# Moving the first top-16 tile into the last units of a local attention

## The chip, the cores and the metric

One core of one Trainium2 chip. The metric is the device time in microseconds of one execution of the whole kernel; below is better. The kernel is one program of five instruction queues: TensorE (PE in the profile; its weight loads are PEld), VectorE (DVE), ScalarE (ACT), GpSimd (POOL) and SyncE (SP), which wait for each other by semaphores set by hand.

## What is computed

Two batches of 1024 tokens with 256 features go through four blocks: a cross-attention, a mixture of experts, a global attention block with an MLP, and a last block. Only the last one matters here. Cut to its core:

```python
h = _ln(x) * (1 + sc_msa) + sh_msa
h = _self_attn(h, ...)            # windows of 128 tokens, rolled by 64; 16 heads of 16
x = x + h * g_msa
h = _ln(x) * (1 + sc_mca) + sh_mca
h = _topk_cross_attn(h, context, ...)
x = x + h * g_mca
h = _ln(x) * (1 + sc_mlp) + sh_mlp
x = x + _swiglu(h, ...) * g_mlp

# in _topk_cross_attn: 64 context tokens, 16 heads, TOPK = 16
scores = einsum('bqhd,bkhd->bhqk', q, k) / sqrt(D)
top_s, top_i = jax.lax.top_k(scores, TOPK)
attn = softmax(top_s); o = einsum('bhqk,bhqkd->bqhd', attn, vg)
```

## The kernel before, in words

A batch is two blocks of 512 tokens (k = 0, 1), each of four tiles of 128 tokens, so eight tiles t. PSUM has eight banks. Every engine's program is written out in its order by hand; an engine runs its instructions in that order, and a wait stops all that stands behind it on that engine.

**Local attention.** There are 16 units, u = 2 t + c: a window of 128 tokens and half of the heads. For a unit TensorE makes the scores minus the row maxima (`window_scores`, L1179 and L1182, banks 4 to 7), ScalarE their exponential (`window_exp`, L1710), TensorE the products with the values and the sums (`window_values(u - 1)`, L1197, banks 2 and 3), and VectorE divides (`window_divide`, L2312 and L2313). For units up to 6, token scores and row maxima of unit u + 9 (`window_tokens`, `window_maximum`) run between these. `window_scores(u)` waits for the exponential of unit u - 1; `window_values(u)` waits for its own exponential and for the division of unit u - 2.

When units 0 to 7 are divided, block 0 is complete. TensorE then multiplies it with the output weights (`projection`, L627 and L632, after the values of unit 8), VectorE adds it to x (`residual`, L1989) and takes mean and variance (`statistics`, L1895 to L1900) in its round 10, GpSimd takes the root (L2464), VectorE normalises (`normalise`, L1907) in round 11, TensorE turns the result (`ln`, L600) after unit 13, ScalarE evicts it with scale and shift (`ln`, L1412), and TensorE makes block 0's queries (`query`, L464) after unit 15's scores; ScalarE evicts those too. VectorE builds the key matrix of the top-16 attention (`build_keys(2)`, L2004 to L2007) in round 13. Block 1 goes the same way after the units.

**Top-16 attention.** For tile t, TensorE makes the scores against the block-diagonal keys (`top_scores`, L1254, banks 0 and 1); ScalarE copies them (`top_copy`, L1729) into one of the three buffers of `prob3`; VectorE takes the largest eight of each head with 16 MAX8 (`best`, L2346), marks them with 16 MATCH_REPLACE8 (`mark`, L2351), takes the next eight (`next_best`, L2358) and marks those (`mark_next`, L2363). Once the first are marked, GpSimd subtracts each head's maximum (`centre`, L2582), ScalarE takes the exponential (`exp`, L1733), and VectorE masks it with the marks (`mask`, L2369). TensorE turns the tile (`top_turn`, L1267), ScalarE evicts (`turned`, L1740), TensorE multiplies with the values (`top_values`, L1274), and VectorE divides (`divide`, L2014 and L2017), one tile later.

In the kernel before all of this comes after the units: VectorE's division of unit 15, then `best(0)`. Around tile 0 VectorE also has block 1's residual, statistics (after `mark(0)`) and normalisation (after `next_best(0)`), TensorE block 1's projection, turning and queries, and ScalarE their evictions, with `exp(0)` ahead of them and `exp(1)` behind.

`keep_busy(bank, n)` issues n matmuls of 128x512 whose result nobody reads (L592). From tile 4 on the MLP's matmuls are laced into the tiles (`up`, L1299, `down`, L1326); after tile 7 the second half of the MLP follows.

In SBUF `prob3` is three buffers of 4 KB; the first two lie over the second half of `kp3`, the keys that the units of block 1 read, the third lies behind it.

## Time and profile before

| | |
|---|---|
| three runs, median (lowest to highest) | 1666.86 us (1666.84 to 1670.57) |
| the profiled execution | 1668.83 us |
| its span, first to last instruction | 1666.8 us |
| PE busy, share of the span | 1526.9 us, 92% |
| DVE busy | 1048.8 us, 63% |
| ACT busy | 769.6 us, 46% |
| POOL busy | 379.3 us, 23% |
| chain that ended last, by engine | PE 68%, DVE 19%, issue 6%, ACT 4%, DMA 1%, POOL 1% |
| mean granted TensorE clock | 0.969 |

The chain is followed back from the last instruction, at each step to what released it; its shares say where the end was set, while busy time only says how full an engine is. "Issue" is time in which the engine waited for nothing that the profile shows. A busy PE is not PE at its peak. In batch 0 the units run from about 622 to 678 us and the tiles from 681 to 795 us; in batch 1 both come some 802 us later.

### The profile page before, as it was taken

The page shows a single profiled execution, that of the slowest core. Times are in us where ns is not written, and L with a number is a line of the kernel's source. Part 1 is how long each engine was busy: PE and PEld are TensorE (multiplying, and loading weights), DVE is VectorE, ACT ScalarE, POOL GpSimd, SP SyncE. Part 2 cuts the span into 40 slices and gives each one's busy share as a digit, 9 for nine tenths or more (in the row PEclk, how much of TensorE's full clock was granted, in tenths as well). Part 3 has the DMA queues.
Part 4 walks back from the last instruction along what each step waited for, and adds up shares of the span by engine and source line. Part 5 has one row for each costly group of instructions (what it writes and reads, how often), then busy time and mean ns, then how long its engine had stood idle before and what let it go on. Part 6 is the DMA issues. An engine that isn't in the chain of part 4 may idle for free.

```text
span 1666.8 us, 26374 instructions
## 1 busy us (share of the span) xinstructions
PE 1526.9 (92%) x10485; PEld 926.8 (56%) x10485; DVE 1048.8 (63%) x2946; ACT 769.6 (46%) x1228; POOL 379.3 (23%) x419
## 2 busy tenths in 40 slices
PE   5899998999998999878998999899999899987898
PEld 3447674444354857556764767444444475655676
DVE  3573344999627445899357334499982734579953
ACT  1334421688843533325443443148885354333444
POOL 3510006342016010114133000434400701001320
PEclk9899999999999999999999899999999999999999
DMA  9400017221020000000130000632202000000000
GB/s 336 143 1 0 0 41 147 36 40 26 2 76 1 1 1 3 1 1 1 56 109 1 0 1 0 161 49 40 40 2 77 1 1 1 3 1 1 1 1 26
DMA packets 37551, 59.60 MB, mean 36 GB/s; under 512 B 7360, under 2 KB 26980, under 8 KB 36532
## 3 DMA queue, kind: packets, MB, share of 16 engines
q1 hardware_dynamic: 25239, 34.71, 6.3%
q0 software_dynamic: 9408, 15.85, 6.2%
q10 hardware_dynamic: 2780, 7.36, 1.3%
q8 instruction: 82, 1.34, 0.3%
q14 instruction: 42, 0.34, 0.1%
HBM read 42.03 MB, written 2.10 MB: 26 GB/s over the span
## 4 chain that ended last, share of the span: by engine, by line
PE 68%; DVE 19%; issue 6%; ACT 4%; DMA 1%; POOL 1%; ACTq 0%; DVEq 0%; POOLq 0%
PE ps L993 9%; PE ps L1005 8%; PE ps L464 7%; PE ps L1299 4%; PE ps L978 3%; PE ps L870 3%; PE ps L1092 3%; DVE taken L2351 3%; PE ps L1100 3%; DVE rs L2036 2%; PE ps L848 2%; PE ps L592 2%; DVE mxw L2028 2%; PE ps L600 2%; PE ps L1156 2%
## 5 line engine op out<-in xcount | busy, mean ns | idle before, releaser
L2221 DVE TENSOR_REDUCE mm<-ps 128x1 f32<-128x1024 f32 x256 | 310.1, 1222 | 32.8 <-PE ps L978 25.6
L1618 ACT ACTIVATE pt<-ps 128x512 f32<-128x512 f32 x512 | 276.7, 600 | 59.1 <-PE ps L993 42.4
L2464 POOL TENSOR_TENSOR rstd<-ve,minus_half 128x4 f32<-128x4 f32 x32 | 35.7, 1114 | 745.0 <-DVE ve L1900 745.0
L993 PE MATMUL ps<-qx,kx 64*128 64x512 f32 x512 | 188.3, 445 | 1.0 <-ACT pt L1618 1.0
L978 PE MATMUL ps<-kx,qx 48*128 48x512 f32 x512 | 186.6, 444 | 0.2
L1005 PE MATMUL ps<-pt,v 128*32 128x256 f32 x2048 | 158.7, 390 | 0.0
L993 PEld LDWEIGHTS ps<-qx,kx 64*128 64x128 f32 x512 | 79.0, 184 | 95.9 <-ACT pt L1618 85.9
L2111 DVE TENSOR_TENSOR rlo<-ring,rhi 128x512 fp32r<-128x512 f32 x48 | 33.2, 692 | 121.6 <-ACT ring L1568 121.5
L1005 PEld LDWEIGHTS ps<-pt,v 128*32 128x32 f32 x2048 | 42.9, 108 | 85.5 <-ACT pt L1618 60.4
L978 PEld LDWEIGHTS ps<-kx,qx 48*128 48x128 f32 x512 | 75.4, 184 | 22.0 <-issue 18.0
L592 PE MATMUL ps<-filler 128*128 128x512 f32 x262 | 83.6, 434 | 0.0
L2510 POOL DMA_DIRECT2D qx<-mxT x64 | 33.3, 527 | 200.1 <-ACT mxT L1610 180.0
L1568 ACT ACTIVATE rhi<-ps,mod 128x512 fp32r<-128x512 f32 x48 | 33.0, 688 | 96.0 <-PE ps L779 95.9
L1989 DVE TENSOR_TENSOR x<-x,ps 128x512 f32<-128x512 f32 x64 | 41.3, 681 | 40.2 <-PE ps L616 27.5
L1412 ACT ACTIVATE hT<-ps,mod 128x512 f32<-128x512 f32 x48 | 34.7, 775 | 67.5 <-PE ps L600 67.5
L600 PE MATMUL ps<-ident,xhat 128*128 128x128 f32 x256 | 39.4, 296 | 26.9 <-DVE xhat L1907 23.6
L2305 DVE TENSOR_REDUCE mxw<-ps 128x8 f32<-128x1024 f32 x32 | 38.8, 1223 | 39.2 <-PE ps L1156 39.2
L2582 POOL TENSOR_TENSOR prob<-prob,m 128x1024 f32<-128x1024 f32 x16 | 31.0, 1936 | 142.5 <-DVE taken L2351 142.5
L1710 ACT ACTIVATE wprobT<-ps 128x1024 f32<-128x1024 f32 x32 | 32.7, 1023 | 61.1 <-PE ps L1182 60.9
L2028 DVE TENSOR_REDUCE mxw<-ps 128x16 f32<-128x1024 f32 x32 | 37.7, 1219 | 36.4 <-PE ps L650 36.4
L592 PEld LDWEIGHTS ps<-filler 128*128 128x128 f32 x262 | 44.8, 188 | 27.8 <-issue 22.3
L1907 DVE TENSOR_SCALAR xhat<-x,mv,rstd 128x256 f32<-128x256 f32 x128 | 46.3, 424 | 19.5 <-POOL rstd L2464 19.3
(373 smaller groups left out, 3397.5 us busy)
## 6 DMA issues: line engine op xcount, KB each, us to landing
wm<-in_L_xcond_W_mlp_dram SPq DMA_DIRECT2D x4, 1024.0 KB, 8.3
qx<-q_hi POOLq DMA_DIRECT2D x64, 64.0 KB, 2.6
kx<-k_hi POOLq DMA_DIRECT2D x64, 64.0 KB, 2.8
w3a<-in_L_xcond_w_m_dram SPq DMA_DIRECT2D x2, 2048.0 KB, 8.2
w<-in_L_xcond_e_w_dram SPq DMA_DIRECT2D x6, 512.0 KB, 6.9
w<-in_L_xcond_e_w_dram SPq DMA_DIRECT2D x2, 1536.0 KB, 13.6
s_ada<-in_L_xcond_w_ada_dram ACTq DMA_DIRECT2D x1, 2304.0 KB, 24.3
qx<-q_lo POOLq DMA_DIRECT2D x32, 64.0 KB, 2.6
```

The source lines that it names most:

```text
L464: ins = pe.matmul(ps[:, bank, :], w[:, c, m * P:(m + 1) * P], src[:, c, :], start=c == 0, stop=c == KC - 1)
L592: pe.matmul(ps[:, bank, :], filler[:, 0:P], filler[:, :], start=True, stop=True)
L600: ins = pe.transpose(ps[:, bank + c, t * P:(t + 1) * P], xhat[:, TB * k + t, c * P:(c + 1) * P], ident[:, :])
L870: ins = pe.matmul(ps[:, 6 - 2 * (j % 2) + c, :], w_[:, m, c * P:(c + 1) * P], part, start=n % 4 == 0 and i == 0, stop=n % 4 == 3 and i == 2)
L978: ins = pe.matmul(ps[:, bank + half, :], qx[r, p % 4, t * P:(t + 1) * P], kx[r, p % 4, half * 512:(half + 1) * 512], start=True, stop=True)
L993: pe.matmul(ps[:, bank, :], kx[r, p % 4, kc * P:(kc + 1) * P], qx[r, p % 4, half * 512:(half + 1) * 512], start=True, stop=True).then_inc( ...
L1005: ins = pe.matmul(ps[o:o + 32, 7, q:q + BLK // 2], v2[:, kc, VS * (2 * p + e):VS * (2 * p + e) + 32], pt[:, (2 * kc + e) % 8, half * BLK + ...
L1092: ins = pe.matmul(ps[:, m % 4, :], w1s[:, wp, c, m * P:(m + 1) * P], hs[:, k, sp, c, :], start=(wp, sp, c) == (0, 0, 0), stop=(sp, c) == ( ...
L1299: ins = pe.matmul(ps[:, 4 + i, :], w3ap[wp][:, c, (NC_HID * i + m) * P:(NC_HID * i + m + 1) * P], src[:, c, :], start=(wp, part, c) == (0, ...
L1618: act.activation(pt[:, u % 8, half * 512:(half + 1) * 512], ps[:, bank, :], ACT.Exp, scale=QK_SCALE).then_inc(st_read, 1)
L2028: ins = dve.tensor_reduce(mxw[:, t, :].rearrange("p (r n) -> p r n", r=4)[:, :, 0:4], ps[:, bank:bank + 4, o:o + D].rearrange("p r (h s) - ...
L2221: return dve.tensor_reduce(mm[:, p % 2, e, t:t + 1], place(), X, ALU.max).then_inc(ring_read, 1)
```

## The change

On TensorE: `top_scores` is defined ahead of the units. Block 0's projection stands ahead of `window_values(8)` in place of behind it, block 0's turning after unit 11 in place of 13, its queries after unit 12 in place of 15, and the scores of tile 0 after unit 13. After the units come the scores of tile 1, then block 1's projection, then the scores of tile 2; block 1's turning and queries stand behind the values of tile 0. Unread matmuls: 10 and 8 around block 1's projection, 5 and 4 around its turning, in place of 8 ahead of it, in bank 6 in place of 3.

On ScalarE: evictions follow, `top_copy(0)` stands after unit 13's exponential, and `exp(1)` ahead of the eviction of block 1's queries.

On VectorE: the rounds of the units end at 13. Block 0's residual and statistics come in round 9 ahead of the division of unit 8, the keys in round 8, the normalisation in round 10. Then `best(0)`; the division of unit 13; `mark(0)`; those of units 14 and 15; the rest of tile 0; block 1's residual and statistics after `mask(0)`, and its normalisation after `best(1)`.

On all: tile t lies in buffer (t + 2) % 3 of `prob3` in place of t % 3.

```diff
 # TensorE
                     window_scores(u)
                     if u + 9 < N_UNIT:
                         window_tokens(u + 9, 0)
+                    if u == 9:
+                        projection(R_B_SA, 0, wso, oT, 0, (None, (wo_ready, u0 + N_UNIT // 2), None))
                     if u:
                         window_values(u - 1)
                     if u + 9 < N_UNIT:
                         window_tokens(u + 9, 1)
                     if u == 7:
                         window_turn_maxima(1)
-                    elif u == 9:
-                        projection(R_B_SA, 0, wso, oT, 0, (None, (wo_ready, u0 + N_UNIT // 2), None))
+                    elif u == 11:
+                        ln(6, 0, bank=0)
+                    elif u == 12:
+                        query(2, 0, 14, wq3, bank=0)
                     elif u == 13:
-                        ln(6, 0, bank=0)
-                query(2, 0, 14, wq3, bank=0)
+                        top_scores(0)
                 window_values(N_UNIT - 1)
...
-                top_scores(0)
+                top_scores(1)
+                keep_busy(6, 10)
                 projection(R_B_SA, 1, wso, oT, 4, (None, (wo_ready, u0 + N_UNIT), None))
-                top_scores(1)
-                keep_busy(3, 8)
-                ln(6, 1)
-                query(2, 1, 14, wq3)
+                top_scores(2)
+                keep_busy(6, 8)
                 for t in range(TB):
                     if t:
                         top_scores(t + 2)
...
                     top_turn(t)
+                    top_values(t)
                     if t == 0:
-                        top_scores(2)
-                    top_values(t)
+                        keep_busy(6, 5)
+                        ln(6, 1)
+                        keep_busy(6, 4)
+                        query(2, 1, 14, wq3)
 # ScalarE
                     if u == 7:
                         window_maxima(1)
+                    elif u == 11:
+                        ln(6, 0, (mod, M3_SC_CA, M3_SH_CA), 0)
+                    elif u == 12:
+                        query(2, 0, C_BQ3C, 0)
                     elif u == 13:
-                        ln(6, 0, (mod, M3_SC_CA, M3_SH_CA), 0)
-                query(2, 0, C_BQ3C, 0)
+                        top_copy(0)
...
-                top_copy(0)
                 top_copy(1)
                 exp(0)
+                top_copy(2)
+                turned(0)
                 ln(6, 1, (mod, M3_SC_CA, M3_SH_CA))
+                exp(1)
                 query(2, 1, C_BQ3C)
-                turned(0)
-                top_copy(2)
                 for t in range(1, TB):
                     outputs3(t - 1)
-                    exp(t)
+                    if t > 1:
+                        exp(t)
                     top_copy(t + 2)
                     turned(t)
 # VectorE
-                for u in range(N_UNIT):
+                for u in range(N_UNIT - 2):
                     if u + 9 < N_UNIT:
                         window_maximum(u + 9)
+                    if u == 9:
+                        link(residual(5, 0, 0))
+                        statistics(b, 6, 0)
                     if u:
                         window_divide(u - 1)
-                    if u == 10:
-                        link(residual(5, 0, 0))
-                        statistics(b, 6, 0)
-                    elif u == 11:
+                    if u == 8:
+                        build_keys(2)
+                    elif u == 10:
                         normalise(b, 6, 0)
-                    elif u == 13:
-                        build_keys(2)
-                window_divide(N_UNIT - 1)
...
                     best(t)
                     if t == TB + 1:
                         add(0, 4)
+                    elif t == 0:
+                        window_divide(N_UNIT - 3)
+                    elif t == 1:
+                        normalise(b, 6, 1)
                     mark(t)
                     if t == 0:
-                        link(residual(5, 1))
-                        statistics(b, 6, 1)
+                        window_divide(N_UNIT - 2)
+                        window_divide(N_UNIT - 1)
...
                     next_best(t)
-                    if t == 0:
-                        normalise(b, 6, 1)
                     if t and t not in (TB, TB + 1):
                         divide(t - 1)
                     mark_next(t)
                     mask(t)
+                    if t == 0:
+                        link(residual(5, 1))
+                        statistics(b, 6, 1)
```

## Rows read from the trace of the kernel before

**Rows 1.** Busy time by stretch, VectorE alone: stretch, length, busy (instructions), clock, DMA, GB/s.
```profile
681.14:711.07 29.93, 28.59 (x212) 0.89 0.00 1
1483.00:1513.17 30.17, 28.58 (x211) 0.83 0.00 1
```
**Rows 2.** Waits of VectorE, 681 to 795 us: total us, times, longest.
```profile
DVE prob L2369 <- ACT prob L1733: 0.5, 1, 0.5
DVE rs L2014 <- PE ps L1274: 0.3, 1, 0.3
```
**Rows 3.** Timeline of VectorE, batch 0: start us, length us, instructions [idle before <-releaser].
```profile
660.79 0.96 DVE L2312 RECIPROCAL rs<-ps 128x128 f32<-128x128 f32 x1 [5.14 <-PE ps L1197]
...
661.99 1.27 DVE L1989 TENSOR_TENSOR x<-x,ps 128x512 f32<-128x512 f32 x2
...
665.22 0.95 DVE L2312 RECIPROCAL rs<-ps 128x128 f32<-128x128 f32 x1
...
670.12 1.28 DVE L2004 TENSOR_TENSOR kblk<-kT,head_mask 128x512 f32<-128x512 f32 x2
...
681.14 2.12 DVE L2346 MAX8 m<-prob 128x8 f32<-128x64 f32 x16 [1.77 <-ACT prob L1729]
...
718.73 0.26 DVE L2014 RECIPROCAL rs<-ps 128x16 f32<-128x16 f32 x1
```
**Rows 4.** Timeline of TensorE's matmuls, batch 0.
```profile
654.22 0.73 PE L627 MATMUL ps<-row_hl,row_of 64*128 64x512 f32 x2
...
658.54 0.50 PE L1179 MATMUL ps<-qT,kp 32*128 32x128 f32 x8
...
659.64 0.65 PE L1197 MATMUL ps<-wprobT,v 128*32 128x128 f32 x16
...
660.85 0.50 PE L1179 MATMUL ps<-qT,kp 32*128 32x128 f32 x8
...
673.31 3.70 PE L464 MATMUL ps<-hT,wq 128*128 128x512 f32 x8
...
677.96 1.98 PE L1254 MATMUL ps<-kblk,qT 128*128 128x512 f32 x4
...
685.40 2.42 PE L592 MATMUL ps<-filler 128*128 128x512 f32 x8
692.52 1.76 PE L600 MATMUL ps<-ident,xhat 128*128 128x128 f32 x8 [4.70 <-DVE xhat L1907]
695.15 6.06 PE L464 MATMUL ps<-hT,wq 128*128 128x512 f32 x8 [0.87 <-ACT hT L1412]
...
743.66 5.41 PE L632 MATMUL ps<-wco,oT 128*128 128x256 f32 x16
...
754.85 3.49 PE L1254 MATMUL ps<-kblk,qT 128*128 128x512 f32 x4
```
**Rows 5.** Timeline of ScalarE, batch 0.
```profile
679.98 1.03 ACT L1729 ACTIVATE prob<-ps 128x1024 f32<-128x1024 f32 x1 [2.24 <-PE ps L1254]
...
688.55 1.06 ACT L1733 ACTIVATE prob<-prob 128x1024 f32<-128x1024 f32 x1 [1.52 <-POOL prob L2582]
```
**Rows 6.** Timeline of all engines at an earlier projection, residual and norm.
```profile
485.09 3.72 PE L632 MATMUL ps<-wproj,hT 128*128 128x256 f32 x16
...
487.98 0.69 DVE L1989 TENSOR_TENSOR x<-x,ps 128x512 f32<-128x512 f32 x1 [0.70 <-PE ps L632]
...
489.57 1.38 DVE L1907 TENSOR_SCALAR xhat<-x,mv,rstd 128x256 f32<-128x256 f32 x4
...
491.48 1.08 ACT L1472 ACTIVATE hT<-ps 128x512 f32<-128x512 f32 x2 [10.49 <-PE ps L600]
```
**Rows 7.** Timeline of VectorE, a normalisation beside GpSimd's centring.
```profile
758.39 2.36 DVE L1907 TENSOR_SCALAR xhat<-x,mv,rstd 128x256 f32<-128x256 f32 x4
```
**Rows 8.** Busy time by stretch: stretch, length, busy of PE, PEld, DVE, ACT, POOL, clock.
```profile
640.00:680.00 40.00, 37.49 (x765) 27.82 (x764) 24.46 (x48) 14.59 (x17) 1.01 (x1) 1.00 0.01 2
...
692.00:702.00 10.00, 8.61 (x25) 4.56 (x26) 9.90 (x76) 2.88 (x5) 0.00 (x0) 0.66 0.00 1
```

More of the change, by code:

```diff
@@ L1199, in window_values, with top_scores @@
                     ins.then_inc(wpv_done, 1)
+                t0 = b * T
+                def top_scores(t):
+                    if t % TB == 0:
+                        pe.wait_ge(qT_ready, b * 2 * N_Q + 4 + t // TB + 1)
+                    if t == 0:
+                        pe.wait_ge(kblk_ready, b + 1)
+                    else:
+                        pe.wait_ge(ts_read, t0 + t)
+                    for c in range(KC):
+                        ins = pe.matmul(ps[:, c, :], qT[:, t // TB, c, t % TB * P:(t % TB + 1) * P],
+                                        kblk[:, c, :, :].rearrange("p h s -> p (h s)"), start=True, stop=True)
+                    ins.then_inc(ts_ready, 1)
                 window_linear(0, 0)
@@ L1234, in _ @@
                         window_turn_maxima(1)
-                    elif u == 9:
-                        projection(R_B_SA, 0, wso, oT, 0, (None, (wo_ready, u0 + N_UNIT // 2), None))
+                    elif u == 11:
+                        ln(6, 0, bank=0)
+                    elif u == 12:
+                        query(2, 0, 14, wq3, bank=0)
                     elif u == 13:
-                        ln(6, 0, bank=0)
-                query(2, 0, 14, wq3, bank=0)
+                        top_scores(0)
                 window_values(N_UNIT - 1)
-                t0 = b * T
-                def top_scores(t):
-                    if t % TB == 0:
-                        pe.wait_ge(qT_ready, b * 2 * N_Q + 4 + t // TB + 1)
-                    if t == 0:
-                        pe.wait_ge(kblk_ready, b + 1)
-                    else:
-                        pe.wait_ge(ts_read, t0 + t)
-                    for c in range(KC):
-                        ins = pe.matmul(ps[:, c, :], qT[:, t // TB, c, t % TB * P:(t % TB + 1) * P],
-                                        kblk[:, c, :, :].rearrange("p h s -> p (h s)"), start=True, stop=True)
-                    ins.then_inc(ts_ready, 1)
                 def top_turn(t):
@@ L1266, in top_turn @@
                         for j in range(4):
-                            ins = pe.transpose(ps[:, 2 + half, j * P:(j + 1) * P], prob3[:, t % 3, (4 * half + j) * P:(4 * half + j + 1) * P], ident[:, :])
+                            ins = pe.transpose(ps[:, 2 + half, j * P:(j + 1) * P], prob3[:, (t + 2) % 3, (4 * half + j) * P:(4 * half + j + 1) * P], ident[:, :])
                         ins.then_inc(tp_turned, 1)
@@ L1710, in window_exp, with top_copy @@
                     act.activation(wprobT[:, u % 2, :, :].rearrange("p (r o) q -> p r (o q)", o=2), ps[:, 4:8, 0:2 * P], ACT.Exp, scale=QK_SCALE).then_inc(wp_exp, 1)
+                t0 = b * T
+                def top_copy(t):
+                    act.wait_ge(ts_ready, t0 + t + 1)
+                    if t >= 3:
+                        act.wait_ge(tp_turned, 2 * t0 + 2 * t - 4)
+                    act.activation(prob3[:, (t + 2) % 3, :], ps[:, 0:2, :].rearrange("p a n -> p (a n)"), ACT.Copy).then_inc(ts_read, 1)
                 window_queries_keys(1)
@@ L2416, in _ @@
                     mask(t)
+                    if t == 0:
+                        link(residual(5, 1))
+                        statistics(b, 6, 1)
                 divide(7)
```

15 lines of the change are left out of this document (4 added, 11 removed).

## The prediction

> **What bounds the kernel now.** I read the chain of waits first: by its shares (in the table above) TensorE and VectorE set the time between them, so the question is which of the two sets the pace where the edits are. Then busy time by stretch, VectorE's waits, and each engine's timeline around the change. Each batch ends its local attention with sixteen units and then runs eight top-16 tiles on VectorE. Over the first two tiles (first selection of tile 0 to first selection of tile 2) VectorE is busy 28.6 us of 29.93 in batch 0 and of 30.17 in batch 1 [rows 1]; the remainder is overhead between instructions and few waits. From tile 0 to the end of tile 7 it has two other waits in batch 0, 0.5 us for the exponential of tile 1 and 0.3 us for tile 0's value products [rows 2]. So from tile 0 on VectorE is the path, and everything behind it (tiles 2 to 7, the MLP, the next batch) starts when it lets go. Ahead of tile 0 it is not: it idles 5.14 us before one unit's division [rows 3]. There TensorE and ScalarE are the path: scores, exponential, values, 2.31 us a unit (660.85 - 658.54) [rows 4].
>
> The gain is therefore the shift of one event, the first selection of tile 2 (711.07 us in batch 0). The shift has two parts: how much earlier tile 0 starts, and how much work VectorE gains or loses between there and tile 2.
>
> **When tile 0's scores come.** I walk TensorE's new order from the scores of unit 9, which nothing before the edit moves. Before, that unit's scores and the values of unit 8 precede the projection at 654.22, 2.2 us together, so they begin at about 652.1.
> - A half step (16 matmuls of scores or of values) is 1.10 us: scores at 658.54, values at 659.64 [rows 4]. The projection takes 4.32 us, from 654.22 to the next scores at 658.54.
> - Unit 9: scores to 653.2; the projection, now ahead of the values, to 657.5 (it needs unit 7's division, which follows that unit's values, issued before 652.1, by 1.15 us and lasts 1.20: done at about 653.3); values of unit 8 to 658.6.
> - Unit 10: bound by the exponential, 660.85 - 658.54 = 2.31, to 660.9. Unit 11: two half steps, to 663.1.
> - The norm's transposes, moved from unit 13 to unit 11. VectorE: the residual's first add starts 2.89 us into the projection's 16 matmuls (487.98 - 485.09) [rows 6], here about 656.8; adds and statistics 3.23 (665.22 - 661.99) [rows 3], to 660.0 and with the second add's wait 660.3; the divisions of units 8 and 9, 1.20 each, to 662.7; the normalisation's 1.38 ends at 664.1; 0.53 more to ScalarE's eviction (491.48 against 489.57 + 1.38) [rows 6]: 664.6. TensorE is free at 663.1 and needs about 1.0, so a new wait of 0.4 arises; the next scores start at 664.5.
> - Unit 12: two half steps and the query projection, 3.6 (its row has 3.70, of which the next instruction overlaps a little) [rows 4], to 670.3; ScalarE has evicted the norm's two halves by then. Unit 13: two half steps, 672.5; the top-16 scores, 2.02 to the copy's start (679.98 - 677.96), and 1.16 more to the selection (681.14 - 679.98) [rows 3 to 5]: **675.7**, where it was 681.14. Tile 0 starts 5.4 us earlier. The query's evictions and the copy lie between exponentials on ScalarE, which has over 1 us free in every unit.
>
> The added waits: the values of unit 10 want unit 8's division, done at 661.5, and come at 662.0, so 0.5 us is spare; the last unit's values want unit 13's division, which now stands behind tile 0's first selection, done at 679.1, when unit 15's exponential ends too. Building the keys (moved from unit 13 to unit 8) falls into VectorE's wait for the projection: 1.28 us and two small copies [rows 3] against 3.4 from 653.4 to 656.8. Without that wait it would cost its 1.6 once a batch on the norm's chain.
>
> **What VectorE carries until tile 2.** Three divisions (units 13, 14, 15), which were done before tile 0, now stand inside its chain: 3 x 1.20 = 3.6 us. Residual, statistics and normalisation of the second block only change places. The two waits of [rows 2] go, 0.8 us: tile 1's exponential no longer stands behind two query evictions, and tile 0's values come before the query matmuls. Batch 1 has 0.2 more to lose [rows 1]. From 675.7 the chain is 29.9 + 3.6 - 0.8 = 32.7, to 708.4 or 708.5.
> What must be on time there:
> - tile 0's exponential ended 8.5 us after the first selection's start (688.55 + 1.06) [rows 5]; with one division ahead that is 685.4, and the mask comes near 690.2;
> - the second projection starts when unit 15's division is done, 684.8, and takes 4.3, to 689.2; the residual comes at 691.4 (spare 2.2). Ten unread matmuls ahead of it, 8 of which took 2.42 [rows 4], end before 684.8 too;
> - tile 1's exponential, behind the norm's evictions on ScalarE, at about 704.4 against a mask at 707.4;
> - tile 0's values by 696.5, against their division at 703.6.
> Cost of all four: nothing, and each has 2 us or more to lose first. The query of block 1 now ends near 703.6. At half clock it would end near 706.1, the next tile's turn would slip to 711.3 and its values to 714.9; their division is due 7.66 us after tile 2's selection (718.73 - 711.07) [rows 3], at 716.1: still covered. Of the 27 unread matmuls (8 before), none is on the path then.
>
> **The sum.** Per batch 5.4 - 3.6 + 0.8 = 2.6 us, with 0.2 more in batch 1: 5.4; I take 5.3, by the later of the two readings of tile 2 above. The profiled execution took 1668.83 us for a span of 1666.8; it should become 1663.5. The median of the three runs is 1.97 below it, so by the median: 1666.86 - 5.3 = **1661.6 us**. Unknown ends: the new wait at the norm between 0 and 1.5 us a batch (VectorE's queue against TensorE's), the unit chain otherwise exact to 0.3; below, the two waits may stay (+0.8 a batch). That gives 1660.4 to 1664.8 for this case.
>
> **A collision.** The normalisation took 2.36 us where GpSimd ran the centring at the same time and 1.38 elsewhere [rows 6, 7]. In the new order the centring of tile 1 starts after the normalisation of block 1 (698.1 against 701.4), so I add nothing. The Trainium skill (GPSIMD Engine Reference, Key points) says the two engines share their SBUF interfaces, so that a VectorE instruction reading two SBUF inputs or in a two-port mode contends; the trace agrees. If both batches met it once, 1.0 us each, the sum would come to 1663.6.
>
> **Rivals.**
> - *Slower: the clock falls in the units.* TensorE was granted 1.00 of its clock through the units, and 0.66 in 692 to 702, right after it had idled 4.70 us [rows 4, 8]; the reordered units give it a new pause at the norm. At 1.2 GHz the query takes 6.06 instead of 3.70, the projection 5.41 instead of 3.72, the top-16 scores 3.49 instead of 1.98 [rows 4]: 2.4 + 1.7 + 1.5 = 5.6 us a batch, 1661.6 + 11.2 = 1672.8. It decides beyond a delay of 2.6 us a batch. Against it: the pause is 0.4 us, and TensorE keeps its 37.49 us of 40 or nearly in a stretch that was granted 1.00 [rows 8]. Chance 6%. The Trainium skill (TensorE: Matmul & The Clock Gate, What's actually happening) holds the throttled state to be the default and activity what releases it; by that rule any thinner stretch is a risk, and the trace agrees only for the long pause.
> - *The gain is mostly given back*: the divisions are paid in full but tile 0 starts only 3 to 4 us earlier, because the norm's chain through VectorE, GpSimd and ScalarE ends later than I say, or the collisions above occur. 1 to 3 us gained, 1664 to 1666. For it: six handovers between engines lie in that chain. Chance 27%.
> - *It does not shorten anything*: something behind tile 2 that VectorE's timeline does not show holds the end (a DMA, a split). Against it: VectorE has no wait in tiles 2 to 7. 1666.9, chance 6%.
> - *More*: the norm costs no wait and the second half of each batch meets a better clock, 7 us gained, 1659.9. Chance 8%.
> The forecast has 53%.
>
> **Numbers.** A change of 0.3% (5.0 us, below 1661.9) is about what measuring this kernel can tell from none, and the forecast sits just beyond it. Of its 53% I count 44 below that line, with 8 from the last rival: faster 0.52. Same: the rest, 0.41. Slower by over 0.3% (above 1671.9): the clock rival, with a point for the unforeseen, 0.07. The range leaves out the clock rival and half of both tails: 1659.5 to 1666.5.
>
> **What would show it.** In the new profile of batch 0: the first selection at 675 to 677; three divisions among tile 0's selection and marking; no wait of VectorE for an exponential or value product before tile 7; tile 2's first selection 2.2 to 2.8 us earlier, and the same shift at the end of tile 7; twice that at the end of the span. The forecast is wrong if the unit chain waits over 1 us for the norm, if VectorE waits inside tiles 0 and 1, or if the shift at tile 2 does not reach the end.

## The result and the profile after

| | before | after |
|---|---|---|
| median of 18 executions each | 1666.01 us | 1656.84 us |
| lowest to highest | 1660.26 to 1672.5 | 1650.26 to 1663.1 |
| the profiled execution, its span | 1668.83, 1666.8 | 1657.31, 1655.5 |
| mean granted TensorE clock in it | 0.969 | 0.978 |

The ratio is 0.995, with a 95% interval from 0.9938 to 0.9962: 8.3 us faster by the ratio, 9.2 by the medians. I had predicted 1661.6 us and a range that ended at 1659.5. The direction was right, the size was not, and the question of the experiments was where the 4.8 us beyond the forecast came from. Of these 0.9 are in the starting point: the kernel before has a median of 1666.01 us over 18 executions, and 1666.86 over the three that I had.

First the place that was edited. The timeline of VectorE around tile 0, batch 0, marks left out:

```profile
658.69 0.69 DVE L1998 TENSOR_TENSOR x<-x,ps 128x512 f32<-128x512 f32 x1 [1.82 <-PE ps L632]
...
664.59 1.37 DVE L1916 TENSOR_SCALAR xhat<-x,mv,rstd 128x256 f32<-128x256 f32 x4
...
677.43 2.12 DVE L2354 MAX8 m<-prob 128x8 f32<-128x64 f32 x16 [1.77 <-ACT prob L1723]
679.59 0.96 DVE L2321 RECIPROCAL rs<-ps 128x128 f32<-128x128 f32 x1
...
684.12 0.96 DVE L2321 RECIPROCAL rs<-ps 128x128 f32<-128x128 f32 x1
685.12 0.29 DVE L2322 TENSOR_TENSOR oT<-ps,rs 128x128 f32<-128x128 f32 x1
685.32 0.95 DVE L2321 RECIPROCAL rs<-ps 128x128 f32<-128x128 f32 x1
...
698.49 1.39 DVE L1916 TENSOR_SCALAR xhat<-x,mv,rstd 128x256 f32<-128x256 f32 x4
...
710.29 2.12 DVE L2354 MAX8 m<-prob 128x8 f32<-128x64 f32 x16
```

The three divisions stand inside tile 0's selection, and tile 2's first selection comes at 710.29. That can't be held against 711.07 [rows 3] as it is, because this execution reached the units 1.9 us later than the one of before did. A mark that no edit touches is needed: ScalarE's second copy of row maxima in a batch (`maxW`), at 649.06 us before (first line) and at 650.98 after (second):

```profile
649.06 0.60 ACT L1704 ACTIVATE maxW<-ps 128x512 f32<-128x512 f32 x1 [0.55 <-PE ps L1163]
650.98 0.60 ACT L1709 ACTIVATE maxW<-ps 128x512 f32<-128x512 f32 x1 [0.55 <-PE ps L1163]
```

From that copy to tile 0's selection it is 26.45 us (677.43 - 650.98) against 32.08, to tile 2's 59.31 against 62.01. I call this stretch the **zone**; it holds every edit. The busy time of VectorE by stretch, tile 0 to tile 2 in both batches, answers to [rows 1]; below it are its waits from tile 0 to tile 7, which answer to [rows 2] (batch 1 shows the same single line):

```profile
677.43:710.29 32.86, 32.12 (x218) 1.00 0.01 1
1469.01:1501.85 32.84, 32.10 (x217) 1.00 0.01 1
```

```profile
DVE m L2354 <- ACT prob L1723: 1.8, 1, 1.8
```

The one wait left is that for tile 0's scores, ahead of the stretch. TensorE's timeline answers to [rows 4]:

```profile
655.79 3.72 PE L632 MATMUL ps<-wso,oT 128*128 128x256 f32 x16
...
664.34 0.62 PE L1197 MATMUL ps<-wprobT,ones_win 128*32 128x128 f32 x16
665.05 1.41 PE L600 MATMUL ps<-ident,xhat 128*128 128x128 f32 x8
...
668.50 3.70 PE L464 MATMUL ps<-hT,wq 128*128 128x512 f32 x8
...
674.25 1.99 PE L1212 MATMUL ps<-kblk,qT 128*128 128x512 f32 x4
...
701.24 3.70 PE L464 MATMUL ps<-hT,wq 128*128 128x512 f32 x8
```

The norm's transposes wait for nothing, and the second query takes 3.70 us where it had taken 6.06. Last the whole span in stretches, all engines (length, busy of PE, PEld, DVE, ACT, POOL, granted clock, DMA share, GB/s): start to zone, zone, tiles 2 to 7, the stretch to the next zone, zone, and the rest.

```profile
0.00:650.98 650.98, 601.24 (x4057) 340.58 (x4057) 382.90 (x613) 304.81 (x508) 161.50 (x204) 0.97 0.20 55
650.98:710.29 59.31, 56.80 (x695) 39.51 (x695) 46.66 (x251) 21.68 (x26) 5.89 (x4) 1.00 0.01 2
710.29:791.36 81.07, 63.03 (x314) 47.62 (x315) 79.27 (x609) 34.28 (x47) 23.92 (x15) 0.96 0.00 1
791.36:1442.56 651.20, 618.43 (x4162) 362.18 (x4160) 389.43 (x574) 323.18 (x525) 151.45 (x174) 0.99 0.14 35
1442.56:1501.85 59.29, 56.77 (x695) 39.51 (x695) 46.63 (x250) 21.69 (x26) 5.88 (x4) 1.00 0.01 2
1501.85:1655.50 153.65, 127.97 (x602) 97.88 (x602) 104.49 (x654) 64.94 (x96) 30.24 (x19) 0.96 0.02 8
```

The stretch between the zones, from batch 0's last mask to batch 1's maxima copy, holds no edit, and took 658.80 us before:

```profile
792.11:1450.91 658.80, 625.95 (x4162) 366.04 (x4160) 389.31 (x574) 323.02 (x525) 151.72 (x174) 0.98 0.14 34
```

The same 4162 matmuls keep TensorE busy for 618.43 us instead of 625.95: 7.5 us less, the whole 7.6 of the stretch. So the profiled 11.3 us divide as follows: zones 2.70 + 2.97 = 5.67, between them 7.6, and 1.9 given back at the start, which had more half-clock time than before (41 us against 34).

The half-clock time of a stretch is the sum of the pieces in which the granted clock stood at 1.2 GHz instead of 2.4. It follows from the mean clock: 0.9895 over 651.2 us (rounded to 0.99 above) is 14 us of it, 0.9767 over 658.8 is 31.

### The profile page after: what moved, and what is told of

Its sections match the earlier page's. It is cut to its first block, busy times and chain, and to the rows that moved or that the text cites. A ratio compares the mean times of both kernels' runs of the same rounds, so it can differ in the third digit from the quotient of the medians.

```text
span 1655.5 us, 26452 instructions
## 1 busy us (share of the span) xinstructions
PE 1524.2 (92%) x10523; PEld 927.3 (56%) x10523; DVE 1049.4 (63%) x2946; ACT 770.6 (47%) x1228; POOL 378.9 (23%) x419
## 4 chain that ended last, share of the span: by engine, by line
PE 65%; DVE 22%; issue 6%; ACT 3%; SPq 1%; POOL 1%; DMA 1%; DVEq 0%; POOLq 0%; ACTq 0%
PE ps L993 9%; PE ps L1005 9%; PE ps L464 6%; PE ps L1302 4%; DVE taken L2359 3%; PE ps L978 3%; PE ps L870 3%; PE ps L1092 3%; PE ps L1100 3%; DVE taken L2371 3%; DVE rs L2045 2%; PE ps L848 2%; DVE m L2354 2%; DVE mxw L2037 2%; PE ps L592 2%
## 5 line engine op out<-in xcount | busy, mean ns | idle before, releaser
L1623 ACT ACTIVATE pt<-ps 128x512 f32<-128x512 f32 x512 | 276.8, 599 | 59.1 <-PE ps L993 41.4
L592 PE MATMUL ps<-filler 128*128 128x512 f32 x300 | 94.5, 433 | 0.0
L1005 PEld LDWEIGHTS ps<-pt,v 128*32 128x32 f32 x2048 | 42.9, 108 | 85.7 <-ACT pt L1623 61.6
L592 PEld LDWEIGHTS ps<-filler 128*128 128x128 f32 x300 | 51.6, 188 | 29.9 <-issue 23.3
L2045 DVE RECIPROCAL rs<-ps 128x512 f32<-128x512 f32 x16 | 53.7, 3355 | 7.3 <-PE ps L687 7.3
```

The lines of the kernel that those rows point to most:

```text
L592: pe.matmul(ps[:, bank, :], filler[:, 0:P], filler[:, :], start=True, stop=True)
L1005: ins = pe.matmul(ps[o:o + 32, 7, q:q + BLK // 2], v2[:, kc, VS * (2 * p + e):VS * (2 * p + e) + 32], pt[:, (2 * kc + e) % 8, half * BLK + ...
L1623: act.activation(pt[:, u % 8, half * 512:(half + 1) * 512], ps[:, bank, :], ACT.Exp, scale=QK_SCALE).then_inc(st_read, 1)
L2045: link(dve.reciprocal(rs2[:, u % 2, :], ps[:, bank + 1, :]))
```

## The experiments

Two theories stood. **Theory of the edits**: all of the gain comes from the changed order, the unread matmuls or their aftermath. **Theory P**: the edits give the zones' 5.67 us, and the rest depends on where half-clock pieces fall in code that nobody changed; these move when a stretch begins a little earlier or later. In the expectations the first is also called the rival. Those of e1 to e4 were written before theory P had its name and use letters of their own: S is that the edits give the zones' gain and half clock elsewhere the rest, C that the unread matmuls bring part of the gain. The runs were timed in jobs beside the kernel before, which came to medians of 1665.73 (29 executions, e1 to e4), 1666.05 (34, e5 to e8), 1666.71 (11, e9 to e12) and 1668.36 (11, e13 to e15). "Zones" are the two times from the maxima copy to tile 2; "between" is the unedited stretch.

| kernel | median us | ratio to before | zones us | between us (half clock) |
|---|---|---|---|---|
| before | 1666.01 | | 62.0, 62.3 | 658.8 (31) |
| after | 1656.84 | 0.995 [0.9938, 0.9962] | 59.3, 59.3 | 651.2 (14) |
| e1 no unread matmuls | 1657.21 | 0.9967 [0.9948, 0.9985] | 59.3, 59.3 | 651.3 (14) |
| e2 tile 0 late | 1666.16 | 1.0005 [0.9981, 1.0029] | 61.6, 61.6 | 661.8 (37) |
| e3 padded 2.75 us | 1668.23 | 1.0012 [0.9996, 1.0028] | 62.1, 62.1 | 658.9 (31) |
| e4 exponential only | 1684.04 | 1.0105 [1.0083, 1.0128] | 68.1, 68.1 | 661.8 (37) |
| e5 before + 0.5 us | 1662.44 | 0.9971 [0.9959, 0.9983] | 62.8, 62.4 | 651.2 (14) |
| e6 after + 0.5 us | 1663.53 | 0.9975 [0.9959, 0.9992] | 59.8, 59.3 | 657.6 (27) |
| e7 after + 1.0 us | 1666.3 | 0.9983 [0.996, 1.0006] | 60.4, 59.3 | 653.4 (17) |
| e8 before + fill | 1670.2 | 1.0019 [1.0007, 1.0032] | 61.3, 61.3 | 661.9 (37) |
| e9 after + MLP fill | 1654.65 | 0.9939 [0.9921, 0.9957] | 59.3, 59.3 | 654.2 (17) |
| e10 before + MLP fill | 1659.25 | 0.9957 [0.994, 0.9973] | 62.6, 61.9 | 656.1 (24) |
| e11 before again | 1668.29 (one) | | 62.2, 62.2 | 658.9 (31) |
| e12 after again | 1661.36 (one) | | 59.3, 59.3 | 660.3 (37) |
| e13 after timed | 1659.89 | 0.9938 [0.9921, 0.9954] | 59.2, 59.2 | 654.7 (20) |
| e14 as e9, again | 1656.19 | 0.9917 [0.9903, 0.9931] | 59.2, 59.2 | 655.1 (20) |
| e15 e1 + MLP fill | 1655.28 | 0.9915 [0.9892, 0.9939] | 59.2, 59.1 | 657.6 (27) |

The last two columns come from one profiled execution each, which need not lie at the median: e2's took 1673.83 us, 7.7 above its median.

### The parts of the change

**e1: the change without the unread matmuls at block 1's norm.**

```diff
-                keep_busy(6, 10)
-                keep_busy(6, 8)
-                        keep_busy(6, 5)
-                        keep_busy(6, 4)
```

> The changed kernel without the 27 unread matmuls around block 1's projection and norm. Theory S (schedule): the change itself saves 2.7 and 2.9 us between unit 8 and tile 2, all on VectorE's chain; the rest of the measured 8 to 9 us is half-clock stretches of TensorE that happened to fall on other stages. Then the unread matmuls are beside the path: from the scores of unit 8 to tile 2's first selection stays within 0.5 us of the changed kernel in each batch, and the time within 1 us of its 1656.8 on average. Theory C (clock): the unread matmuls hold TensorE's clock up and bring the missing 3 us; without them the time is about 1660 and the queries of block 1 take 6 us.

The zones stay at 59.29 us, although TensorE is now at half clock for nearly half of the 22 us around the norm (a mean of 0.77) and takes 5.54 us for the query. Busy time by stretch, all engines, and a row of TensorE's timeline:

```profile
690.00:712.00 22.00, 18.28 (x70) 12.50 (x70) 21.58 (x151) 8.07 (x12) 2.94 (x2) 0.77 0.00 0
```

```profile
699.48 5.54 PE L464 MATMUL ps<-hT,wq 128*128 128x512 f32 x8 [0.87 <-ACT hT L1413]
```

VectorE is busy 21.58 of 22 us, so TensorE is not on the path there. In the zones the 27 unread matmuls are neither cost nor gain, as the prediction had it; for the whole execution the two ratios, 0.9967 and 0.995, have intervals that overlap.

**e2: the change with tile 0 late** (its scores, copy and first selection behind the units, and all divisions ahead of it, as before).

```diff
-                    elif u == 13:
-                        top_scores(0)
                 window_values(N_UNIT - 1)
+                top_scores(0)
...
-                for u in range(N_UNIT - 2):
+                for u in range(N_UNIT):
...
+                window_divide(N_UNIT - 1)
```

> The changed kernel, but with tile 0's scores, copy and selection behind the units, and all divisions ahead of them, as before the change. Projection, norm and queries of block 0 stay early, exponential of tile 1 and unread matmuls stay too. Theory S: tile 0 starts 0.3 to 0.5 us later than in the kernel before (same work on TensorE plus the wait for the norm), 0.8 us of waits inside tiles 0 and 1 are gone: unit 8 to tile 2 is 61.0 us against 61.3 before and 58.6 changed, the time 1665 to 1666. Theory C: 3 us below the kernel before, 1663.

Tile 0 comes at 32.30 us from the copy and tile 2 at 61.57. This separates the terms. From tile 0 to tile 2 it takes 29.3 us with the divisions ahead and 32.86 with them inside: the three divisions cost 3.6. The kernel before took 29.93 and 30.17 [rows 1] for what takes 29.3 here: the waits that went are worth 0.7 and 0.9. And tile 0's head start is 32.30 - 26.45 = 5.85 us. The median is that of before, although the zones are still 1.1 us shorter (62.01 + 62.26 - 2 x 61.6). The profiled execution spans 5.2 us more than that of before: 3.0 in the between stretch, with 37 us of half clock, 2.2 in tiles 2 to 7 and 1.1 at the start. Whether the others lost it in the same places no profile shows.

**e3: the change with 2.75 us more work on VectorE behind tile 1, in both batches.**

```diff
                     mask(t)
+                    if t == 1:
+                        link(dve.memset(pad[:, 0, :], 1.0))
+                        for i in range(1, 4):
+                            dve.reciprocal(pad[:, i, :], pad[:, 0, :])
```

> The changed kernel with a memset and three reciprocals of 128x128 more on VectorE between tiles 1 and 2, 3.1 us a batch, so that everything behind tile 2 comes about when it came before. Theory S: VectorE's chain carries the end, so all 6.2 us return: 1663, and 1666 if the other stages meet the half-clock stretches as they did before the change. Theory C: the unread matmuls' share stays, 1660 to 1663. If VectorE were not the path: 1657.

Zones 62.06 and 62.05: all of the padding is paid, which shows VectorE as the path. But against the changed kernel it cost 11.4 us of median (10.3 by the ratios to before, which were taken in different jobs) and not 5.5, and the between stretch is back at 658.9. This was the first sign of theory P: the length of an unedited stretch had followed the edit.

**e4: the kernel before with tile 1's exponential ahead of the query evictions, and nothing else.**

```diff
+                exp(1)
                 query(2, 1, C_BQ3C)
                 turned(0)
...
-                    exp(t)
+                    if t > 1:
+                        exp(t)
```

> The kernel before with one line moved: tile 1's exponential ahead of the eviction of block 1's queries on ScalarE. Theory S: the wait of 0.45 us for it at tile 1's mask goes, the queries' eviction comes 1 us later and turning tile 0 with it; unit 8 to tile 2 shrinks by 0 to 0.5 us a batch, the time is 1665 to 1666. Theory C says the same, since no unread matmul is added.

A miss. The zones grew by 6 us. VectorE's timeline shows a wait in tile 1 that neither kernel has, and ScalarE's, below it, shows the cause:

```profile
708.60 0.26 DVE L2016 RECIPROCAL rs<-ps 128x16 f32<-128x16 f32 x1 [6.80 <-PE ps L1274]
```

```profile
690.78 1.45 ACT L1412 ACTIVATE hT<-ps,mod 128x512 f32<-128x512 f32 x2 [4.71 <-PE ps L600]
701.57 1.06 ACT L1733 ACTIVATE prob<-prob 128x1024 f32<-128x1024 f32 x1 [9.34 <-POOL prob L2584]
702.53 1.25 ACT L1412 ACTIVATE qT<-ps,colT 128x512 f32<-128x512 f32 x2
703.67 1.08 ACT L1740 ACTIVATE probT<-ps 128x512 f32<-128x512 f32 x2
704.63 1.04 ACT L1729 ACTIVATE prob<-ps 128x1024 f32<-128x1024 f32 x1
```

The exponential waits 9.34 us for GpSimd's centring, which needs VectorE's marks. Behind it stand tile 0's turned eviction and tile 2's copy, so tile 0's values and their division come late. In the changed kernel the same exponential waits too, 3.18 us, but those two stand ahead of it and VectorE does not wait:

```profile
705.03 1.06 ACT L1741 ACTIVATE prob<-prob 128x1024 f32<-128x1024 f32 x1 [3.18 <-POOL prob L2595]
```

### Where the rest came from

**e5: the kernel before with one memset of 0.5 us on VectorE behind tile 1, in batch 0 only.**

```diff
                     mask(t)
+                    if t == 1 and b == 0:
+                        dve.memset(pad[:, 0:512], 0.0)
```

> The kernel before, with one memset of 512 columns (about 0.5 us, an estimate from the 0.96 us of a reciprocal over 128 x 128) added on VectorE behind the masking of tile 1, in batch 0 only. Theory P (the length of the 651 to 662 us between batch 0's last mask and batch 1's second maxima copy depends on where the half-clock stretches of TensorE fall in it, and those move when the stretch begins a little earlier or later): work is added, yet the stretch may shrink from 658.8 to about 651 us, with less than 30.7 us of half clock in it, and the profiled span be up to 7 us shorter than 1666.8. Rival (the stretch is 7.6 us shorter after the change because of the edits themselves): the stretch stays at 658.8 and the span grows by 0.5 us. The zones themselves: batch 0's 62.0 becomes 62.5, batch 1's stays near 62.3.

Work is added and the kernel is faster: 1662.44 against 1666.05 us, with the interval of the ratio wholly below 1. VectorE's timeline shows the memset, and busy time by stretch, all engines, gives the between stretch the changed kernel's length to 0.01 us:

```profile
711.78 1.23 DVE L2370 SCALAR_TENSOR_TENSOR prob<-taken,prob 128x1024 f32<-128x1024 f32 x1 [0.45 <-ACT prob L1734]
713.07 0.48 DVE L2419 MEMSET pad<- 128x512 f32 x1
```

```profile
794.48:1445.69 651.21, 618.38 (x4162) 362.13 (x4160) 389.39 (x574) 323.17 (x525) 151.61 (x174) 0.99 0.15 35
```

None of the change's edits is in this kernel, so the edits are not needed for the 651.2. Cut into corresponding stretches, first of the kernel before, then of e5, it shows where:

```profile
900.00:950.00 50.00, 46.33 (x203) 32.68 (x202) 23.41 (x68) 22.54 (x33) 2.01 (x2) 0.92 0.00 1
...
1300.00:1400.00 100.00, 93.62 (x527) 63.69 (x524) 55.35 (x95) 45.10 (x65) 29.90 (x13) 0.97 0.00 1
1400.00:1450.91 50.91, 45.69 (x648) 29.38 (x648) 28.28 (x35) 15.71 (x18) 3.39 (x2) 0.97 0.01 2
```

```profile
902.37:952.37 50.00, 46.32 (x208) 32.59 (x208) 23.48 (x68) 23.89 (x35) 2.01 (x2) 0.97 0.00 1
...
1302.37:1402.37 100.00, 93.18 (x541) 62.94 (x538) 55.76 (x96) 46.41 (x66) 26.74 (x11) 1.00 0.00 1
1402.37:1445.69 43.32, 39.08 (x620) 26.41 (x616) 25.46 (x31) 13.76 (x16) 3.39 (x2) 1.00 0.01 2
```

Three places of batch 1 ran partly at half clock in the one and not (or for less) in the other: the start of the experts, the start of the second MLP, and the first linear layers of the local attention. The gain is not all kept: e5's profiled start took 1.6 us more than that of before and its zones 0.9 more, of which 0.5 is the memset, and its median lies 3.6 us below before, not 7.

**e6 and e7: the changed kernel with one and with two such memsets** (0.5 and 1.0 us, batch 0 only).

> The changed kernel with the same memset of about 0.5 us in batch 0 only. Theory P: batch 0's zone 59.8 instead of 59.3 us, and the stretch between the batches is either 651 us with 13.7 us of half clock, or 658 to 662 us with 30 to 37 us of it; the median of the runs 0.5 us above the changed kernel's if the first, up to 8 us if the second. Rival: 651 us whatever is added, and the time 0.5 us longer.

> The changed kernel with two such memsets (about 1.0 us) in batch 0 only. Theory P: somewhere between an added 0.5 us and the 2.75 us that brought the stretch between the batches back to 658.9 us, it changes from 651 to 658 to 662 us by a jump and not in proportion; the rival expects 651 us here and a time 1.0 us longer.

The first costs 6.7 us of median for 0.5 of work (1663.53 against 1656.84, in different jobs), the second 9.5; by the ratios to before it is 4.2 and 5.5. The profiled between stretches are 657.6 and 653.4 us: not in order of the added work. e7's twelve executions lie from 1655.21 to 1670.96, four within 2 us of the changed kernel's 1656.84 and six at 1668 us and above. Theory P expected a jump with the added work. The profiles do not show that one; what jumps is the time of single executions of one kernel.

**e11 and e12: both kernels once more, unaltered.**

> The kernel before once more, for the spread of one and the same code: the zones of the two batches again at 62.0 to 62.3 us up to tile 2, whatever the half clock does; the stretch between the batches 651 to 662 us, with the half clock in it going with its length. If the zones vary by more than 0.3 us the reading of 5.67 us as the edits' own share is not good.

> The changed kernel once more: tile 2 at 59.3 us behind the maxima copy in both batches, the stretch between the batches 651 us or, in an execution above 1660 us, 657 us and more with over 20 us of half clock in it.

The zones repeat: 62.18 and 62.18, 59.31 and 59.29. The sum of both, 124.27 before in the first profile and 124.36 here, is good to 0.1 us; how it is split between batches 0.2. The rest does not repeat. The changed kernel's second profile has a start of 644.78 us instead of 650.98 and a between stretch of 660.34 instead of 651.20:

```profile
0.00:644.78 644.78, 593.44 (x4057) 335.48 (x4057) 382.77 (x613) 304.59 (x508) 161.79 (x204) 0.98 0.21 55
786.23:1446.57 660.34, 628.25 (x4162) 367.32 (x4160) 389.51 (x574) 323.14 (x526) 151.78 (x174) 0.97 0.14 34
```

So one profile of each kernel cannot price the unedited code. Start and between together came to 1307.9 and 1307.4 us before, and to 1302.2, 1305.1 and 1305.0 (e13) after.

Tiles 2 to 7 do not always repeat either, though nothing in them was edited. They took 80.8 to 81.3 us in 22 of the 34 batches profiled, and 81.9 to 83.5 in the other 12, in 11 of which VectorE waited 1.7 to 3.0 us for a value product of TensorE's. The changed kernel's second profile has this in batch 0 (82.14 us):

```profile
DVE rs L2023 <- PE ps L1277: 1.7, 1, 1.7
```

The mean granted clock there was 0.92, against 0.96 in its first profile; but e3 had 0.89 and took 81.03 us, so the amount of half clock does not decide it, and what does is open.

Every timed execution has its span and mean clock on record, so the half-clock time of each can be worked out: in 85 executions of the kernel before a mean of 103 us, in 24 of the changed one (its own 18 and e13) 78. In both, a straight line through the executions gives 0.35 us of span for each us of half clock (correlation 0.96 and 0.92). Of the 25 us less, 17 to 20 lay in the zones of before, by its two profiles. That leaves 5 to 8 us outside them, worth 1.6 to 2.8 us by this line, an estimate. With the zones' 5.67 it makes 7.3 to 8.5 us; the means differ by 8.3.

### Why the half clock comes where it does

The second MLP's first 14 long matmuls are the clearest place, since they are one group with two durations. Changed kernel, batch 0 and batch 1 of the same profile:

```profile
533.51 1.41 PE L600 MATMUL ps<-ident,xhat 128*128 128x128 f32 x8 [1.38 <-DVE xhat L1916]
535.87 1.55 PE L1092 MATMUL ps<-hs,w1s 128*128 128x512 f32 x4 [0.96 <-ACT hs L1417]
539.05 6.26 PE L1092 MATMUL ps<-hs,w1s 128*128 128x512 f32 x14 [1.62 <-DVE hs L2271]
...
1331.87 1.55 PE L1092 MATMUL ps<-hs,w1s 128*128 128x512 f32 x4 [0.96 <-ACT hs L1417]
1335.05 3.48 PE L1092 MATMUL ps<-hs,w1s 128*128 128x512 f32 x14 [1.63 <-DVE hs L2271]
```

The same three short pauses (1.38, 0.96 and 1.62 us) stand ahead of both, and the second group ran at 2.4 GHz (granted clock 1.00), the first almost wholly at 1.2 (0.52). The Trainium skill (TensorE: Matmul & The Clock Gate, A second HAM failure mode: psum-queue depth-cycling) tells of a kernel whose TensorE is idle for moments between groups of matmuls often enough that its clock goes back and forth; these rows agree as far as both levels stand behind short pauses, and no run here tests the cause named there, the cycling through PSUM banks. The Trainium skill (TensorE: Matmul & The Clock Gate, What's actually happening) says that what sets the clock runs freely and does not restart with the kernel, so that one kernel differs from execution to execution; the two profiles of the changed kernel (651.20 and 660.34 us between the zones) agree, and no run here controls it.

**e9 and e10: six unread matmuls in the last of the three pauses,** in the changed kernel and in the one before.

```diff
                         if m == 0 and sp == 1:
+                            if k == 0:
+                                keep_busy(1, 6)
                             pe.wait_ge(hs_lo, b * NB + k + 1)
```

> The changed kernel with 6 unread matmuls (about 1.4 us at full clock) in each batch's second MLP, in the 1.6 us in which TensorE waits for the low halves of the hidden tokens. In the profiled execution of the changed kernel the half clock came right there in batch 0 (538 to 545 us) and not in batch 1. Theory P in its stronger form (a short idle time of TensorE decides, when the clock switches at that moment): no half clock there in either batch, the batch some 2.8 us shorter where it had been (14 matmuls of w1s in 3.5 us instead of 6.3), and the median 0 to 3 us below that of the changed kernel, unless later stretches take up the half clock instead. Rival: the idle time there has nothing to do with it, the half clock stays at 538 to 545 us and the time is the same.

> The same 6 unread matmuls in the kernel before, where the profiled execution has the half clock there in batch 1 (1338 to 1345 us) and not in batch 0. Theory P: the stretch between the batches' zones keeps its other half-clock stretches and loses nothing in batch 0; batch 1's MLP is 2.8 us shorter, the median 0 to 3 us below 1666. Rival: 1666.

e10 is 7 us faster than before, 1659.25 against 1666.71 us. Its batch 1, in which the profile of before has 6.30 us:

```profile
1330.57 1.55 PE L1094 MATMUL ps<-hs,w1s 128*128 128x512 f32 x4 [0.96 <-ACT hs L1414]
1331.96 1.52 PE L592 MATMUL ps<-filler 128*128 128x512 f32 x6
1333.75 3.49 PE L1094 MATMUL ps<-hs,w1s 128*128 128x512 f32 x14 [0.26 <-DVE hs L2264]
```

In the 13 profiles without these matmuls, 26 batches, the 14 matmuls took 5.4 to 6.3 us in 20 and 3.5 in 6. In the 4 profiles with them (e9, e10, e14, e15), 8 batches, they took 3.5 in 7 and 4.0 in one, where the half clock had come already in the pause before. In 3 of the 20 it had also come before the last pause. So half clock comes at these pauses in about three of four executions of this place, and filling the last of them prevented it there in 7 of 8. My expectation had the saving as 2.8 us where it had been, that is 2 x 0.77 x 2.8 = 4.3 us a run; e10 gave 7.5 (its executions had 17 us less half clock than those of before in the same job, 85 against 102), e9 2.2 against another job's 1656.84, and what else the half clock did in each is not separated.

**e13, e14 and e15: the changed kernel timed again, with the MLP's unread matmuls, and with these instead of the norm's.**

> The changed kernel timed again: 1657 us median, 8 to 10 us below the kernel before in the same job. Below 6 us would say that the earlier difference was partly luck of the draw.

> The changed kernel with 6 unread matmuls in each second MLP, timed again: 1654 to 1656 us, 1 to 3 us below the changed kernel, if the idle time there decides whether the half clock comes; the same as the changed kernel to 1 us if the earlier 1654.65 us was chance.

> The changed kernel without the 27 unread matmuls at block 1's norm and with 6 at each second MLP. The zones stay at 59.3 us. If only what stands ahead of a stretch that is bound by TensorE matters, 1654 to 1658 us as e14; if the norm's unread matmuls shelter what follows, 1657 to 1660 us, with 20 us of half clock in the two zones as without them.

The changed kernel is 8.5 us below before, as in the first measurement (8.3 by the ratio). With the MLP's unread matmuls the medians are 3.7 us lower in the same job, but the intervals of the ratios overlap. Over all executions, of several jobs, 11 with them have a mean of 1655.2 and 25 of the changed kernel 1658.0: 2.9 us less, with a standard error of 1.0. That is likely a version faster than both, not one that is measured as finely as the change itself. e15 has the same median within what six executions tell: the norm's unread matmuls give nothing here either.

**e8: the kernel before with 24 unread matmuls instead of 8 at block 1's norm,** over the pause of 4.70 us [rows 4].

```diff
-                keep_busy(3, 8)
+                keep_busy(3, 24)
```

> The kernel before with 24 unread matmuls instead of 8 ahead of block 1's norm, so that TensorE has work through the 4.7 us in which it waits for the normalised values. If the half clock of the query that follows (6.06 us in batch 0 where the full clock takes 3.70) came from that idle time, the query takes about 3.7 us now. Both theories expect it to be worth little: the sum of the prediction put no more than 0.3 to 0.8 us of a batch's zone on it, so tile 2 at 61.2 to 62.0 us behind the maxima copy instead of 62.0 and 62.3. What the median does beyond that is the half clock elsewhere: theory P allows plus or minus some 5 us, the rival 1 us at most.

The query takes 3.70 us, and the only wait of VectorE from tile 0 to tile 2 is the one ahead of it:

```profile
694.93 3.70 PE L464 MATMUL ps<-hT,wq 128*128 128x512 f32 x8 [0.87 <-ACT hT L1412]
```

```profile
DVE m L2346 <- ACT prob L1729: 1.8, 1, 1.8
```

So both waits of [rows 2] are gone although nothing was reordered, and tile 0 to tile 2 takes 29.24 and 29.23 us, as in e2 (29.3). The waits came of the old order and the half clock together: e8 takes away the half clock and keeps the order, e1 does the reverse, and neither has them. The zones fell by 0.7 and 1.0 us, the upper end of what I had allowed, and the median rose by 4 (one of the twelve executions took 2405.42 us, for which no profile shows a reason). In the profiled execution tiles 2 to 7 took 3.2 us more over both batches, and the between stretch 3.1 (661.9 us with 37 us of half clock). A saving of 1.6 us in the edited place came with a larger loss in unedited ones, as in e5 with the other sign; that the one caused the other is not shown.

## Why the prediction was wrong, point by point

- **Tile 0's start.** Predicted 675.7, that is 26.6 us from the maxima copy. Measured 26.45 in both batches: 5.63 us earlier, where the prediction had 5.4. The wait at the norm that I had put at 0.4 us did not arise: the values ahead of the transposes ended at 664.96 and these started at 665.05, while the normalisation still ran (664.59 to 665.96). I had let them start only after it.
- **Three divisions inside the chain.** Predicted 3.6; 3.6 by e2.
- **Two waits gone.** Predicted 0.8; 0.7 and 0.9 by e2. The reason given, the place in the queues, is one of two: e8 loses them in the old order, by full clock alone. The prediction saw the half clock of that query and did not ask whether the waits came of it.
- **Unread matmuls and the query of block 1 free.** Right, by e1, and at half clock too.
- **No collision on the normalisation.** It took 1.39 us (698.49), and GpSimd's centring came behind it.
- **From tile 2 to the last mask.** Predicted unchanged. 81.04 and 81.07 us before, 81.07 and 81.05 after; in the second profile of the changed kernel 82.14 and 81.10, for a wait that the forecast does not have.
- **Sum of the zones.** Predicted 5.3, measured 5.67, in every profile of the changed kernel within 0.3.
- **The sum.** The step that failed is "it should become 1663.5": it let the shift at tile 2 reach the end of the span unchanged, and with that held the unedited 1300 us as fixed. They moved by 5.7 us in the profiled pair (1307.9 to 1302.2). By medians the kernel gained 9.2 us: 5.67 from the zones, and a rest of 3.5 from unedited code, of which the count of half clock over all timed executions explains some 1.6 to 2.8.
- **The range.** It was built from errors in the edited place alone. The executions of the unaltered kernel before already lay from 1660.26 to 1672.5 us, and the three of which I knew within 4 us. Its terms, if they all add up, also reach to 1666.0 and not to 1664.8 (2.2 for the norm's wait, 0.6 for the units, 1.6 for the two waits). The pieces at half clock were in the clock's row, and I had priced one only as a loss ("the clock falls in the units") and one as a gain of 1.5 us. Of the rivals, "More: the second half of each batch meets a better clock" was nearest in kind, with 8% and 1659.9 us. The place was right in part: of the three places of batch 1 with less half clock, two lie in its second half (1338 and 1403 us), one at its start (918), and batch 0 up to its zone had more of it.
- **The price of half clock.** The prediction reads 6.06, 5.41 and 3.49 us as durations at 1.2 GHz. The mean granted clocks of these three pieces of the profile before are 0.60, 0.68 and 0.55, so each ran partly at 2.4. Wholly at half clock they would take some 7.4, 7.4 and 4.0 us, twice their full-clock rows (an estimate), and the clock rival would have cost 9.4 us a batch and not 5.6. It did not happen: the granted clock was 1.00 in both zones.
- **"What would show it"**: the signs of the zone came, if its times are taken from the maxima copy (the first selection at 677.43 us as it stands is outside 675 to 677, and tile 2 came only 0.8 us earlier, because of the later start), but "twice that at the end of the span" did not: 11.3 us instead of 5.4.

What stays open: which part of the 3.5 us is lasting, and why there is less half clock outside the zones. Theory P says that it depends on the moment at which each stretch begins, and half to one microsecond of added work went with 3.6 us less of median in e5 and 4 to 9 more in e6 and e7; but no run sets that moment by itself, so it is not shown that the changed kernel's place is a good one for any reason other than chance. What is shown is that the edits are not needed for it (e5) and do not secure it (e6, e7, e12).

## What to carry to other kernels

Price an edit in a zone between two marks that it does not touch, and compare the zones of several profiles; here that repeated to 0.3 us while the span of the same kernel moved by 4. Where TensorE has short pauses ahead of a long group of matmuls, look at that group's duration in more than one profile: if it has two values, a few unread matmuls in the pause may be worth more than a rearrangement. And allow in the range for what the clock does elsewhere: with half a microsecond of added work this kernel was 3.6 us faster in one version and some 4 to 7 slower in the other (e5, and e6 against another job).

## What the runs showed of the hardware

- The same 14 matmuls of 128x512 took 3.48 us (granted clock 1.00) or 6.26 us (0.52) in two batches of one execution, behind the same pauses of 1.38, 0.96 and 1.62 us.
- Six unread matmuls (1.52 us) in the last pause left them at 3.5 us in 7 of 8 batches, where it had been 6 of 26.
- In the changed kernel's zone, where VectorE is the path, half clock costs nothing: e1 has 10 us of it in each zone, the change none, and the zones are equal to 0.02 us. In the old order it cost 0.7 and 1.0 us (before against e8, which has none).
- Over whole executions, each us at half clock went with 0.35 us of span (85 executions of before, 24 of the changed kernel).
- A stretch of 4162 matmuls that no edit touches took 651.20 and 660.34 us in two profiled executions of one kernel. With a 0.48 us memset added in the kernel before, its median fell by 3.6 us.
